# Filler products around the layer norms, and the output gate's projection moved ahead of the block inversion

## The reference, cut to what matters

```python
h = _layernorm(x) * (1 + ca) + sa
x = x + ga * L0_attn(h)            # softmax attention
h = _layernorm(x) * (1 + cb) + sb
x = x + gb * L0_ffn(h)             # top-2 of 8 experts
h = _layernorm(x) * (1 + ca) + sa
x = x + ga * L1_attn(h)            # the gated delta net, below
h = _layernorm(x) * (1 + cb) + sb
x = x + gb * L1_ffn(h)
# L1_attn, per token, with state S:
S = S * exp(gt);  kv = kt @ S;  delta = (vt - kv) * bt
S = S + outer(kt, delta);  ot = qt @ S
g = hidden @ Wg
o = ot * rsqrt(mean(ot^2) + 1e-5) * g_norm_weight
out = (o * g * sigmoid(g)) @ Wo    # g * sigmoid(g) is the output gate
```

## Time and profile before

| | |
|---|---|
| median of 3 runs | 3197.47 us (3193.08 to 3208.31) |
| the profiled execution's own time | 3211.07 us |
| its span, first to last instruction | 3209.3 us |
| mean granted clock of PE over the span | 0.854 |
| busy: PE, DVE, ACT, POOL | 2456.3, 1848.3, 1579.3, 933.0 us |
| chain of work that ended last | PE 32%, issue 31%, ACT 17%, DVE 13%, POOL 5% |

### The profile page before, as it was taken

How to read it: one execution, slowest core, us unless ns; L and a number is a source line. 1 busy time by engine, 2 the same in 40 slices (tenths; PEclk the granted TensorE clock), 3 DMA queues, 4 the chain that set the end, 5 groups by cost and what they waited for, 6 DMA issues and landing times.

```text
span 3209.3 us, 64254 instructions
## 1 busy us (share of the span) xinstructions
PE 2456.3 (77%) x23258; PEld 1762.2 (55%) x23258; DVE 1848.3 (58%) x4392; ACT 1579.3 (49%) x3528; POOL 933.0 (29%) x641
## 2 busy tenths in 40 slices
PE   4868877688776887778877787777877778776787
PEld 2537655376544664446644566445764456544665
DVE  4376563765547554576545664456654666546665
ACT  0475343854447454474535644356443654436544
POOL 2054220533115330153302433034320442204422
PEclk8888888988888888888888888888888888888888
DMA  7101030000300112000210102101121010210102
GB/s 217 41 7 18 9 137 4 11 14 17 129 4 11 15 46 99 4 15 13 88 59 1 16 15 85 58 1 16 16 83 58 3 15 15 83 58 3 17 14 86
DMA packets 232956, 128.45 MB, mean 40 GB/s; under 512 B 177884, under 2 KB 220260, under 8 KB 225668
## 3 DMA queue, kind: packets, MB, share of 16 engines
q1 hardware_dynamic: 227792, 118.11, 13.2%
q10 hardware_dynamic: 4836, 6.03, 0.6%
HBM read 86.95 MB, written 37.11 MB: 39 GB/s over the span
## 4 chain that ended last, share of the span: by engine, by line
PE 32%; issue 31%; ACT 17%; DVE 13%; POOL 5%; DMA 1%; SPq 1%; ACTq 0%; DVEq 0%; POOLq 0%
PE bank L864 4%; PE bank L874 3%; PE bank L930 3%; ACT arena L1651 2%; ACT arena L1540 2%; ACT arena L1541 2%; ACT vq L1548 2%; PE bank L844 2%; PE bank L951 2%; PE bank L847 2%; PE bank L899 2%; PE bank L659 1%; DVE small L1274 1%; PE bank L787 1%; PE bank L668 1%
## 5 line engine op out<-in xcount | busy, mean ns | idle before, releaser
L1226 DVE SCALAR_TENSOR_TENSOR arena<-bank,conv,arena 128x510 f32<-128x510 f32 (+1 forms) x384 | 285.3, 748 | 70.3 <-ACT arena L1541 47.0
L1787 POOL TENSOR_TENSOR arena<-arena 128x511 f32<-128x511 f32 x192 | 243.7, 1271 | 204.1 <-DVE arena L1226 204.0
L1795 POOL TENSOR_TENSOR arena<-upto,gk 128x1536 f32<-128x1536 f32 x32 | 88.1, 2755 | 688.3 <-DVE beta L1219 688.3
L730 PE MATMUL bank<-h_t,arena 128*128 128x512 f32 x384 | 226.8, 686 | 57.3 <-DVE arena L1226 57.1
L1082 DVE TENSOR_REDUCE mx<-bank 128x2 f32<-128x768 f32 (+3 forms) x187 | 202.8, 1124 | 69.9 <-PE bank L517 68.4
L1626 ACT COPY u<-bank 32x192 f32<-32x192 f32 x128 | 39.8, 311 | 410.0 <-PE bank L864 408.5
L1839 POOL TENSOR_TENSOR arena<-arena 128x1536 f32<-128x1536 f32 x24 | 82.5, 3436 | 433.1 <-ACT arena L1643 291.8
L516 PE MATMUL bank<-vq 128*128 128x512 bf16 (+3 forms) x544 | 145.1, 359 | 68.7 <-DVE mx L1082 35.0
L1504 ACT ACTIVATE arena<-bank 128x384 f32<-128x384 f32 (+1 forms) x384 | 167.6, 556 | 56.7 <-PE bank L572 56.0
L787 PE MATMUL bank<-vq 64*128 64x128 f32 x1536 | 114.7, 300 | 57.6 <-ACT arena L1615 36.5
L1525 ACT ACTIVATE arena<-bank,b1e 128x512 f32<-128x512 f32 x128 | 88.0, 687 | 134.5 <-PE bank L659 130.0
(11 more groups left out here) (290 smaller groups left out, 6289.3 us busy)
## 6 DMA issues: line engine op xcount, KB each, us to landing
vq<-q_rows SPq DMA_DIRECT2D x18, 1024.0 KB, 9.4
vq<-k_rows SPq DMA_DIRECT2D x18, 1024.0 KB, 11.2
arena<-w_bounce SPq DMA_DIRECT2D x16, 1024.0 KB, 8.2
q_rows<-qkp SPq DMA_DIRECT2D x81, 128.0 KB, 2.4
k_rows<-qkp SPq DMA_DIRECT2D x81, 128.0 KB, 2.4
arena<-in_L_attn_Wv_dram SPq DMA_DIRECT2D x8, 768.0 KB, 11.1
t<-t_bounce SPq DMA_DIRECT2D x256, 12.0 KB, 1.8
x<-t_bounce SPq DMA_DIRECT2D x256, 12.0 KB, 1.8
```

The costliest lines, as they stand in the source:

```text
L730: mm(ps[:, :], wconv[:, n * P:(n + 1) * P], h_t[:, :], start=True, stop=True).then_inc(z_ps, 1)
L1226: ins = V.scalar_tensor_tensor(a[:, k:T], ps[:, 0:T - k], conv[:, n, 3 - k:4 - k], a[:, k:T], ALU.mult, ALU.add)
L1787: G.tensor_tensor(acc[:, n % 4, 1:T], acc[:, n % 4, 1:T], acc2[:, n % 3, 0:T - 1], ALU.add).then_inc(taps_added, 1)
```

## The change

It has two parts. The first adds filler products: `keep_warm` multiplies a bf16 mask of 512 columns by the identity, into a bank that nobody reads, with no wait of its own. They stand ahead of the transposes of three norms (22, 24 and 12 of them), 4 behind each of these transposes, 10 in the scores at the start of a round, 4 ahead of the last chunk's transposes, and 2 behind each of the last four score units.

The second part moves the gate. For chunks 0 to 2 its products and its silu now stand ahead of the `levels` of the next chunk; that of chunk 3 takes the place where that of chunk 2 was. The gate has its own buffer: `ogt` for chunks 0 to 2, `bm2` for chunk 3. Its banks are 6, 7 and 2 (chunk 3: 3, 6 and 7).

```diff
-        gate = og
+        def gate(c):
+            return ogt if c + 1 < NT else bm2
...
-            return PS[2:5] if c + 1 < NT else PS[0:3]
+            return [PS[6], PS[7], PS[2]] if c + 1 < NT else [PS[3], PS[6], PS[7]]
...
+            if c:
+                stages.append(("gate", c - 1))
             stages.append(("levels", c))
...
-                stages += [("enter_stats", 1), ("rms", c - 1), ("enter_norm", 1), ("enter_h", 1), ("gate", c - 1)]
+                stages += [("enter_stats", 1), ("rms", c - 1), ("enter_norm", 1), ("enter_h", 1), ("gate", c)]
             elif c:
-                stages += [("rms", c - 1), ("gate", c - 1)]
+                stages.append(("rms", c - 1))
...
-        stages += [("rms", NT - 1), ("gate", NT - 1), ("scale", NT - 1), ("project", NT - 1)]
+        stages += [("rms", NT - 1), ("scale", NT - 1), ("project", NT - 1)]
...
+            def keep_warm(bank, n):
+                for _ in range(n):
+                    mm(PS[bank][:, :], ident_bf[:, :], mask_k[:, :, :].rearrange("p h w -> p (h w)"), start=True, stop=True)
...
                 def layer_norm(k):
+                    bank, n = {1: (7, 22), 2: (5, 24), LEAVE: (7, 12)}[k]
+                    keep_warm(bank, n)
                     transpose_norm(b, k)
+                    keep_warm(bank, 4)
...
                 move_maxima(0)
+                keep_warm(5, 10)
                 for u in range(NU + 2, NU + 6):
                     scores(b, 0, u)
...
                     for g in range(NG):
-                        if c + 1 == NT and g == 0:
-                            pe.wait_ge(o_ready, at(b, o_ready, NG * NT))
-                        elif c + 1 < NT and g == 2:
-                            pe.wait_ge(lv_sb, at(b, lv_sb, L_SB * (c + 1) + 4 * NL + 1))
+                        if c + 2 < NT and g == 2:
+                            pe.wait_ge(gd_ready, at(b, gd_ready, NG * (c + 3)))
+                        elif c + 2 == NT and g == 2:
+                            pe.wait_ge(o_ready, at(b, o_ready, NG * (c + 1)))
+                        elif c + 1 == NT and g == 0:
+                            pe.wait_ge(wo_done, at(b, wo_done, c - 1))
+                        elif c + 1 == NT and g == 1:
+                            pe.wait_ge(gate_ready, at(b, gate_ready, NG * c))
...
-                        pe.wait_ge(gate_ready, at(b, gate_ready, NG * c))
+                        pe.wait_ge(gate_ready, at(b, gate_ready, NG * (c if c + 1 < NT else NT)))
...
                 def project(c):
+                    if c + 1 == NT:
+                        keep_warm(7, 4)
...
                 for u in range(7, NU):
                     scores(b, 1, u)
+                    keep_warm(7, 2)
...
+                            pool.wait_ge(og_ps, at(b, og_ps, NG * c))
+                            G.tensor_tensor(og[:, hs, :], ob[:, hs, :], gate(c)[:, hs, :], ALU.mult).then_inc(og_ready, 1)
```

More of the change, by code:

```diff
@@ L754, in keys @@
                         pe.wait_ge(s_ready, at(b, s_ready, 2 * (c - 2) + 1))
+                        pe.wait_ge(gate_ready, at(b, gate_ready, NG * (c - 2)))
                     to_rows(c, NP, kt_ps, k_banks(c))
@@ L767, in mask @@
                             pe.wait_ge(q_sq, at(b, q_sq, 2 * (c + 1)))
-                        elif c >= 3:
-                            pe.wait_ge(gate_ready, at(b, gate_ready, NG * (c - 3) + g + 1))
                         ps = l_banks(c)[g]
@@ L1642, in gate_silu @@
                         act.wait_ge(gt_ps, at(b, gt_ps, NG * c + g + 1))
-                        A.activation(gate[:, GH * g:GH * (g + 1), :].rearrange("p h v -> p (h v)"), gate_banks(c)[g][:, :], ACT.Silu).then_inc(gate_ready, 1)
+                        A.activation(gate(c)[:, GH * g:GH * (g + 1), :].rearrange("p h v -> p (h v)"), gate_banks(c)[g][:, :], ACT.Silu).then_inc(gate_ready, 1)
                     nc.scalar.preload_act_table_set(EXP_LN)
@@ L1838, in scale @@
                         pool.wait_ge(gate_ready, at(b, gate_ready, NG * (c + 1)))
-                        G.tensor_tensor(og, ob, gate[:, :, :], ALU.mult).then_inc(og_ready, 1)
+                        G.tensor_tensor(og, ob, gate(c)[:, :, :], ALU.mult).then_inc(og_ready, 1)
                     else:
@@ L1845, in scale @@
                                 pool.wait_ge(o_ready, at(b, o_ready, NG * NT))
-                            G.tensor_tensor(og[:, hs, :], ob[:, hs, :], gate[:, hs, :], ALU.mult).then_inc(og_ready, 1)
+                            pool.wait_ge(og_ps, at(b, og_ps, NG * c))
+                            G.tensor_tensor(og[:, hs, :], ob[:, hs, :], gate(c)[:, hs, :], ALU.mult).then_inc(og_ready, 1)
                 walk = {"conv": convolve, "mask": mask, "gram": gram, "levels": levels, "scale_v": scale_v, "scan": scan, "rms": rms, "scale": scale,
```

## The result

| | before | after |
|---|---|---|
| median | 3199.02 us (3193.08 to 3208.31, 4 runs) | 3113.80 us (3101.74 to 3123.34, 4 runs) |
| ratio | | 0.9729, 95% interval 0.9687 to 0.9771 |
| profiled execution: span, mean granted clock | 3209.3 us, 0.854 | 3111.0 us, 0.892 |

The kernel is 85 us faster; 61 were predicted. The two traces differ by 98, because the profiled execution of before lies 12 us above its median. The page after, its first lines: PE's busy time grew from 2456.3 to 2521.3 us and the span shrank, so the fillers' work was bought with waiting time.

The account below looks back on a forecast made before the run. PE's waits at the norms leave the clock at 0.50 for the work behind, and around the gate DVE, ACT and POOL wait for PE. Terms sum to 7.6 us per round, 61 by eight rounds: 3197.5 to 3137 us, range 3080 to 3180.

Parts of the forecast that it names:

- First norm, +2.0: First norm: faster products behind the fillers gain 3.65 us, half the rounds pay 2.0 for lateness; 2.0 gained per round.
- start, -0.8: Start of the round: ten fillers where PE waits only 0.51 us delay maxima and scores; 0.8 us lost per round.
- The price of a late filler: First norm: each filler too many delays what follows by 0.215 us, less 0.4 of room, beyond 18 slow ones.
- Second norm, +2.2: Second norm: fillers fit the wait, transposes and products come sooner, ACT's first silu 2.0 to 2.5 us earlier; 2.2 gained.
- last norm, +2.3: Last norm: faster transposes, router and MLP products, of which ACT and DVE take back about 2; 2.3 us gained.
- Second chunk, -1.4: Second chunk: gate 0 moved out leaves PE waiting about 4.6 us, the clock falls, ACT's second scaling ends 1.4 us later.
- Third chunk, +3.9: Third chunk: gate 1 leaves the path; ACT's last scaling ends 3.6 us earlier, inversion's first steps gain 0.3.
- Fourth chunk, first part, -1.5: Ahead of inversion 3: gate 2 takes 2.6 us where the wait is only 0.91; inversion 3 starts 1.5 us later.
- Fourth chunk, end, +0.9: Chunk end: gate 3 and silu leave, scores wait for `k_stack`, start 2.4 us earlier; 0.9 gained, or -0.1 if clock falls.
- the gate's move is worth nothing: Rival: DVE decides in the third chunk or scan 2 runs slow; 3.6 and 0.9 fall away, 3172 us; chance 0.15.

Follow-up runs that it names:

- experiment 3: Changed kernel with 44, 48 and 24 fillers ahead of the three norms' transposes instead of 22, 24 and 12: 3193.66 us, 0.9989 of the kernel before.
- experiment 5: Changed kernel with 12 more fillers ahead of scan 1's key products in the second chunk: 3100.17 us, 0.9696 of the kernel before.
- Experiment 4: Changed kernel with 12 fillers ahead of scan 2, where the gate's six products had stood: 3100.42 us, 0.9707 of the kernel before.

## Why the prediction was right, and where it was not

The time lies in the range, 23 us below the point, and the mechanisms named for the norms and the gate's four places were seen, that of the third chunk in part. By its own terms:

- **First norm, +2.0, and start, -0.8.** The two stages gained 3.1 instead of 1.2. The step that failed is that in half of the rounds the fillers start at the lower clock and end 2.0 us late. In the trace after they end in time in seven of eight rounds (0.37 us of wait left) and 0.3 us late in the first: the clock was up when they began. In the 47 us ahead of these transposes a round has 8.4 us at the lower level before and 1.2 after. Where the fillers do begin at the lower clock, it comes back sooner than the 5 us assumed. That is so in five of eight rounds of the fillers alone, where they end 0.4 to 0.7 us late, as in the third (fillers and transposes, then the window):

```profile
879.91 6.21 PE L482 MATMUL bank<-mask_k,ident_bf 128*128 128x512 bf16 x22
885.96 0.60 PE L487 MATMUL bank<-ident,xn 128*128 128x128 f32 x4
...
879.00:885.00 6.00, 6.00 (x25) 2.96 (x24) 3.90 (x16) 0.50 (x2) 0.00 (x0) 0.72 0.15 44
```

  The price of a late filler was right (experiment 3). A cost of the start's ten is not told by the times.
- **Second norm, +2.2, and last norm, +2.3.** Measured 1.8 and 2.4 behind the transposes and 0.3 each in them, 2.1 and 2.7.
- **Second chunk, -1.4.** Measured -1.0, with the gap (3.96 us, predicted 4.6) and the 0.50 behind it as foretold; experiment 5 fills the gap and takes the 1.0 back. What the Trainium skill's page "TensorE: Matmul & The Clock Gate", section "Why this matters for your kernels", warns of, idle gaps between bursts of matmuls that drop the clock, this gap bears out.
- **Third chunk, +3.9.** Measured 4.0, and that the size fits is in part luck. In the fourth round, from which the term was worked out, the chunk is only 2.7 us shorter (38.72 to 35.97). DVE has its factor 20.4 instead of 21.0 us after inversion 2 began and starts at once, but the rhythm behind it takes 6.9 us instead of 5.4, since the inverse products run at the lower clock. What made up for it was not in the prediction: in six of the eight rounds of before the clock falls on the output products, which makes the chunk 40.2 to 40.3 us long, and after it does not fall there. The third round of before, against 2.94 us in the fourth:

```profile
1149.08 1.77 PE L921 MATMUL bank<-arena 128*64 128x128 f32 x24 [2.14 <-ACT arena L1657]
1150.78 4.37 PE L930 MATMUL bank<-arena 128*128 128x128 f32 x24
```

  Experiment 4 shows that PE's place mattered only up to DVE's.
- **Fourth chunk, first part, -1.5.** Ahead of inversion 3 it is 1.6, as worked out. What the term left out is behind it: 2.2 us less to scan 3's output product. Of this, 0.78 is the silu for which the projections no longer wait; I had read that very wait in the earlier trace rows at gate 1 and not looked for it at gate 2. The rest is the shorter low stretch. The fillers alone have it too, no run shows what shortens it, and to the prediction it is luck.
- **Fourth chunk, end, +0.9.** Measured 0.9, without the 0.3 of the last norm's transposes. The scores wait for `k_stack` as foretold. The clock costs something there in five of eight rounds, where scores and products with Wo take 5.9 to 6.6 us together against 4.4 in the other three, but the products with Wo never take the 5.2 us assumed (3.59 at most). Filled, the stage is 1.1 us shorter than after.

The sum of parts hides one error: the prediction gave the fillers 5.7 us per round (46 us) and the gates 1.9 (15 us). Alone they measured 84 and 25, and beside the fillers the gate's move adds nothing that these runs can tell (0.9723 against 0.9729 and 0.9714). The rival "the gate's move is worth nothing" was thus right about the time that the move adds and wrong about its reason: it gains its 4.0 us in the third chunk and pays for them in the second, ahead of inversion 3 and in clock. Why the two parts together fall 24 us short of their sum (16 by the changed kernel run again) is shown only in part. The mean granted clock says it in every single run: 0.853 to 0.860 for the kernel before, 0.846 to 0.850 with the gates alone, 0.904 to 0.913 with the fillers alone, 0.891 to 0.900 with both. The gate's move lowers the clock, and beside the fillers by more. By the traces it takes 1.0 us per round in the second chunk, and the fillers alone have the short low stretch behind inversion 3 in all rounds, the whole change in four and six of eight. The rest stays open.

## What to carry to other kernels

Fill an engine's wait with work that nobody reads where dense work follows it, and leave some tenths of a microsecond of the wait over: in time it is free, late it costs its full length. When real products are moved out of a place, look at what the gap left there does to the clock, and try fillers in it, up to the moment at which the slowest partner delivers. Here one such gap at a time showed in its stage, by 0.9 to 1.1 us per round, and hardly in the whole time. Measure such edits together and over several runs: single ones that each look good need not add up.

## What had not been expected of the hardware

- The same instructions of inversion 3 have 10.2 us at the lower clock in some rounds and 13.8 in others of one execution (0.68 and 0.57 over 16 us).
- Putting 3.75 us of useless products ahead of scan 2 made the end of that chunk 0.9 us earlier, and so did filling a gap one chunk ahead.
- With three gaps filled the clock fell in another place, on the third chunk's state and output products, in half of the rounds.
- How long PE waits does not tell alone whether the clock falls. Before, a wait of 1.96 us in the second chunk left it up, and behind one of 2.14 us in the third it fell in six rounds of eight.
